# Masked attention on one core: two more groups of a block with three tiles in f16 parts, and VectorE's one-tile gaps on other groups

## What is computed

```python
scores = jnp.einsum('nd,md->nm', x, ks)
scores = jax.nn.leaky_relu(scores, negative_slope=0.2)
scores = jnp.where(adj > 0, scores, -9e15)
attn = jax.nn.softmax(scores, axis=1)
out = layernorm(x + jnp.einsum('nm,md->nd', attn, ks))   # rows of 128, eps 1e-5
```

## Time and profile before

| | |
|---|---|
| median of 3 runs | 1552.41 us |
| profiled execution, own time | 1553.36 us |
| its span, first to last instruction | 1551.6 us |
| granted PE clock, mean | 0.996 |
| busy share of PE, DVE, ACT, POOL | 97%, 97%, 95%, 93% |
| DMA, share of 16 engines | 55.5% |

### The profile page before, as it was taken

The page is one execution under the profiler, slowest core; times in us unless marked ns, Lnnn a source line. Parts: engine busy times, 40 slices in busy tenths (PEclk is TensorE's granted clock), DMA queues, the critical chain, the costliest instruction groups (busy, mean ns, idle before and its releaser), DMA issues.

```text
span 1551.6 us, 43289 instructions
## 1 busy us (share of the span) xinstructions
PE 1502.5 (97%) x16784; PEld 1414.1 (91%) x16784; DVE 1502.6 (97%) x1809; ACT 1475.7 (95%) x1883; POOL 1440.9 (93%) x1245
## 2 busy tenths in 40 slices
PE   5699999999999999999999999999999999999997
PEld 3499999999999999999999999999999999999987
DVE  7999999999999999999999999999999999999984
ACT  6799999999999999999999999999999999999997
POOL 4999999999999999999999999999999999999996
PEclk9999999999999999999999999999999999999999
DMA  9855556555555655555555555655555555555510
GB/s 350 278 194 190 198 197 202 198 188 194 194 192 190 203 190 192 194 192 194 202 191 191 188 187 188 201 183 188 193 190 188 200 182 191 194 188 190 196 63 8
DMA packets 107131, 296.00 MB, mean 191 GB/s; under 512 B 10800, under 2 KB 40240, under 8 KB 106928
## 3 DMA queue, kind: packets, MB, share of 16 engines
q1 hardware_dynamic: 106928, 293.25, 55.5%
HBM read 289.01 MB, written 4.19 MB: 189 GB/s over the span
## 4 chain that ended last, share of the span: by engine, by line
PE 76%; issue 9%; DVE 8%; ACT 5%; POOL 2%; DVEq 0%; DMA 0%; ACTq 0%; POOLq 0%
PE weighted L796 21%; PE scores L748 11%; PE scores L750 11%; PE scores L749 11%; PE weighted L812 7%; PE weighted L808 7%; PE weighted L810 7%; DVE running L654 3%; DVE ring L670 2%; ACT ring L491 2%; DVE ring L640 1%; ACT pt_hi L498 1%; POOL pt_lo L399 1%; ACT scores L484 1%; PE scores L796 0%
## 5 line engine op out<-in xcount | busy, mean ns | idle before, releaser
L394 POOL TENSOR_TENSOR ring<-ring,floor 128x768 f32<-128x768 f32 (+1 forms) x498 | 704.0, 1414 | 48.1 <-ACT floor L511 47.9
L399 POOL TENSOR_TENSOR pt_lo<-ring,pt_hi 128x512 f16<-128x512 f32 (+1 forms) x512 | 658.3, 1286 | 18.1 <-ACT pt_hi L498 17.3
L640 DVE SCALAR_TENSOR_TENSOR ring<-adj_sb,scores 128x1024 f32<-128x1024 int32 x512 | 621.2, 1213 | 6.0 <-ACT scores L484 5.6
L484 ACT ACTIVATE scores<-scores,shrink 128x1024 f32<-128x1024 f32 x512 | 553.6, 1081 | 51.4 <-PE scores L750 46.8
L491 ACT ACTIVATE ring<-ring,lift 128x1024 f32<-128x1024 f32 x512 | 583.6, 1140 | 5.3 <-DVE ring L670 4.0
L748 PE MATMUL scores<-xt_hi,kt_hi 128*128 128x256 f16 x2048 | 560.0, 273 | 25.9 <-DVE ring L640 17.6
L750 PE MATMUL scores<-xt_hi,kt_lo 128*128 128x256 f16 x2048 | 560.5, 274 | 0.0
L749 PE MATMUL scores<-xt_lo,kt_hi 128*128 128x256 f16 x2048 | 560.4, 274 | 0.0
L654 DVE TENSOR_TENSOR running<-ring,running 128x1024 f32<-128x1024 f32 x448 | 547.7, 1223 | 0.1
L796 PE MATMUL weighted<-k_rows,ring 128*128 128x129 f32 x3472 | 472.6, 276 | 2.0 <-DVE y L691 0.9
L796 PEld LDWEIGHTS weighted<-k_rows,ring 128*128 128x128 f32 x3472 | 427.6, 192 | 14.1 <-ACT ring L491 8.1
(11 more groups left out here) (74 smaller groups left out, 544.2 us busy)
## 6 DMA issues: line engine op xcount, KB each, us to landing
adj_sb<-in_adj SPq DMA_DIRECT2D x512, 512.0 KB, 3.4
ring<-in_ks_t SPq DMA_DIRECT2D x8, 512.0 KB, 7.2
x_row<-in_x SPq DMA_DIRECT2D x32, 128.0 KB, 3.5
out<-normed SPq DMA_DIRECT2D x32, 128.0 KB, 3.6
x_probe<-in_x_t SPq DMA_DIRECT2D x29, 128.0 KB, 3.5
xt_raw<-in_x_t SPq DMA_DIRECT2D x29, 128.0 KB, 4.6
ring<-in_ks SPq DMA_DIRECT2D x12, 128.0 KB, 4.8
k_rows<-in_ks SPq DMA_DIRECT2D x12, 128.0 KB, 4.6
```

The source lines that it names most:

```text
L394: nc.gpsimd.tensor_tensor(here, here, below, ALU.subtract).then_inc(gap_ready, 1)
L399: nc.gpsimd.tensor_tensor(pt_lo[:, g % PARTS, 0:QUAD - whole, :], ring[:, g % RING, whole:, :], pt_hi[:, g % PARTS, 0:QUAD - whole, :], AL ...
L640: nc.vector.scalar_tensor_tensor(ring[:, g % RING, :, :], adj_sb[:, g % ADJS, :, :], 0.0, scores[:, g % 2, :, :], ALU.is_le, ALU.subtract)\
```

## The change

Six groups of a block instead of four have three parted tiles: 1, 3, 7, 9, 11 and 15. A block has 38 parted and 26 whole tiles instead of 36 and 28. DVE's one-tile gaps are on groups 0, 5, 8 and 13 instead of 0, 4, 8 and 12. The four portions in which the parts of ks are made follow the table: 10, 9, 10 and 9 tiles instead of 9 each.

```diff
-    WHOLE = [1 if q % 4 == 3 else 2 for q in range(GROUPS)]
+    WHOLE = [1 if q % 8 in (1, 3, 7) else 2 for q in range(GROUPS)]
...
         def dve_tiles(g):
-            return QUAD if g >= ALL - LEFT_OUT else 3 if g >= ALL - GROUPS else min(1 + g % 4, 2)
+            return QUAD if g >= ALL - LEFT_OUT else 3 if g >= ALL - GROUPS else 1 if g % 8 in (0, 5) else 2
...
-                    rows = slice(n * PARTEDS // 4, (n + 1) * PARTEDS // 4)
+                    rows = slice(FIRST_PARTED[4 * n], FIRST_PARTED[4 * n + 4])
```

## The result

The kernel after takes 1558.46 us (median of 6 runs, 1557.94 to 1559.58), the one before, run beside it, 1553.33 us (6 runs, 1552.19 to 1553.93). The ratio is 1.0035, with a 95% interval from 1.0025 to 1.0045: slower by 5.1 us. The prediction was 1552.7 us, no change, and the time lies 2 us above its range (1547.4 to 1556.4). In the profiled execution it took 1558.32 us, with a span of 1556.5 (before 1551.6). The granted clock was 0.995 in the mean, before 0.996. The means are alike, but the two executions have their stretches at the lower clock in different places, and at the end of the program that matters; this is taken up under e6.

A forecast was written before the change was run, and what follows sets the result against it. PE's ring of 46.475 us was taken as the bound, DVE 0.24 behind. Ordinary blocks -0.8, start +0.5 and end +0.6 gave +0.3 us: 1552.7 us on the median, no change, range 1547.4 to 1556.4.

The forecast's parts named there:

- PE's ring: From L683 through a whole block of weigh and score back to L683: 46.475 us, 0.24 longer than DVE's own work.
- the PE step: Two more parted tiles save 0.105 us each in weigh, bringing PE's part of the period to 46.265 us.
- PE, DVE, ACT by themselves: Per block: PE gains 0.21 us, DVE's moved gaps nothing, ACT's longer high parts (0.42 us) hidden by waiting for PE.
- POOL: Two longer low parts cost 0.976 us a block; their lateness lengthens DVE's two-input least, leaving 0.8 us gained of 5.7.
- How late is group 13's low part then?: Overlap of POOL's last low part before the floor wait with DVE's two-input least, put at 0.326 + 46.475 - P.
- P: The period of an ordinary block, from L683 to L683, forecast at 46.45 us.
- PE's lead of 0.21: PE runs 0.21 us ahead of DVE, so the floor starting POOL's next round comes earlier; otherwise the period grows 0.105.
- The start: Two longer low parts in the chain without slack before DVE's first masks: +0.5 us (0 to 0.9).
- The end: After the last mask, where PE waits for POOL's and ACT's longer parts: +0.6 us (0 to 1.2).
- The collision is larger: Slower rival at the two-input least: both unknowns adverse, period 46.68, time 1559.0 us; chance 0.13.
- ACT: Slower rival: masks 7 and 15 wait behind longer high parts, DVE's period 46.66, time 1558.5 us; chance 0.04.
- The gain arrives: Faster rival: POOL's lateness doesn't reach the two-input least, or PE's lead grows; period 46.265, time 1547.8 us; chance 0.23.

The follow-up runs named there:

- e6: The kernel after with L600 (128x3, the last instruction of setting a scale) issued as three of 128x1: 1557.57 us, ratio 1.0024.
- e4: The kernel after, but from the second block on POOL makes only two of three low parts in groups 1 and 9: 1547.64 us, ratio 0.9967.
- e9: e6 with the scaling of each block of x (L365) moved from POOL to ACT: 1550.93 us, ratio 0.9986.
- e7: Against the kernel before: five groups with three parted tiles (1, 3, 7, 11, 15), gaps as before, L600 by columns: 1550.51 us, ratio 0.9981.
- e2: The kernel before with only DVE's one-tile gaps moved to groups 0, 5, 8, 13: 1553.08 us, ratio 1.0000.
- e5: The kernel before, but from the second block on POOL makes three low parts in groups 1 and 9, one unused: 1556.13 us, ratio 1.0021.
- e1: The kernel after with DVE's one-tile gaps on groups 0, 4, 8, 12 as before: 1557.01 us, ratio 1.0030.
- e8: The kernel before with L600 issued as three instructions of 128x1: 1553.81 us, ratio 1.0003.
- e12: e9 with the x scaling of blocks 1 and 2 (counted from 0) left on POOL: 1550.12 us, ratio 0.9985.
- e3: The kernel after, but from the second block on group 1's least takes the running minimum in PSUM instead of group 0 in SBUF: 1549.83 us, ratio 0.9975.

## Why the prediction was wrong

**What bounds the kernel: right.** PE's ring at 46.475 us, DVE just behind: e4 and e9 have the 46.267 that the PE step forecast (46.265), e7 the 46.372 of one tile.

**PE, DVE, ACT by themselves: right.** e2 shows the moved gaps at nothing, e4 the longer high parts of ACT at nothing.

**POOL: the right place and the right mechanism, the sum wrong.** The step that failed is "How late is group 13's low part then?". It counts six terms, overlap = 0.326 + 46.475 - P, and holds DVE by this less 0.14. It lets POOL hold DVE, but not DVE hold POOL. The lengthened `least` ends later, and then overlaps POOL's next gap, which starts 1.19 us after the `least` began, when the floor comes (1188.23 to 1189.42). In the kernel before that was 1.40 (1136.89 to 1138.29), so PE's lead of 0.21 did reach the floor. With s for what the `least` is lengthened by, the gap is longer by (1.225 + s) - 1.19 - 0.14 = s - 0.105. With the measured s = 0.33 that is 0.23: the gap's 2.05 instead of 1.82. This lateness goes once around POOL's round and is there again at the next `least`:

overlap = 0.326 + 46.475 - P + (s - 0.105), and s = overlap - 0.14, so s cancels and P = 46.475 + 0.081 = 46.56 us.

Measured: 46.56. DVE's own 46.235 + s gives s = 0.33, and that too was measured. Read otherwise, two units that exclude each other form one line: POOL's round and the `least` follow each other, and the period is their sum. In my sum half of the excess came back (P stood on both sides and was halved), here none does. That is 0.11 us on P, 27 x 0.11 = 3.0 us of the miss (the 27 periods were put at -0.8 us and came to +2.35). It also shows why the `least` wasn't long in every second block, as I wrote, but about 1.55 in nearly each: a `least` that is longer by s hands on a round that is later by s.

That this second hold makes the rest is read from the traces of after; no experiment took it away alone. The period by itself doesn't tell it from my formula without PE's lead, which gives (93.106 / 2 =) 46.55 us and is what e5 measured; the gap's start at 1.19 us and its 2.05 us do. The trace of before had it too, in the two blocks with a new scale (around 345.8 and 904.9 us), where the gap starts beside the `least`, and I had not looked there:

```profile
345.66 1.22 DVE L654 TENSOR_TENSOR running<-ring 128x1024 f32<-128x1024 f32 x1
345.82 2.73 POOL L394 TENSOR_TENSOR ring<-ring,floor 128x768 f32<-128x768 f32 x1 [1.82 <-ACT floor L511]
```

The `least` still had 1.06 us to run, and the gap took 2.73 us instead of 1.82, 0.91 more.

The Trainium skill (SBUF — State Buffer, Who interferes with whom), which I had cited, has this lock in both directions. It has one line on instructions with two SBUF inputs, as the `least`, and one on DVE's two-port mode, and there it says: "Whoever issues first gets the shared pair for the whole instruction; the other **fully blocks** (not throttle)". I applied it in one direction. The trace agrees in both, but for the 0.14 us in each.

**Left out: L600.** I put the two blocks with a new scale at no change. The three instructions cost 2.3 us more (0.96, 0.69, 0.67), by the same exclusion: in rows before they were already at 0.54 where one column takes 0.21, and I hadn't looked for what else DVE has that a low part can hold. e6 shows the shape as the cause (all at 0.21). The Trainium skill (VectorE: DVE Perf Modes, What auto-detection actually checks) bears on it: a one-source operation from SBUF to SBUF goes in the two-port mode when the outermost non-unit dimensions are both even or equal, as three and three are; 128x1 has no such dimension. The runs agree, though they show the shape and not the mode. One thing differs from "whoever issues first": by the start times of the trace all three L600 began 0.01 to 0.02 us ahead of POOL's low part (345.70 and 345.72), and it was DVE that was held.

**The start** was put at +0.5, for POOL's longer low parts; without L600 it is 1.74 - 0.96 = +0.78. But e1 has these low parts too, and its first L683 is only 122.44 - 122.08 = 0.36 later, 0.24 of it by L600. So the low parts alone cost 0.1 there, and the size came near only together with the moved gaps, which alone (e2, 122.35) cost 0.3 at most. **The end** was put at +0.6 and came to -0.46. That was no fault of the term: at a clock of 1.00 the stretch takes 77.75 us with the work of before (e2) and 78.58 now, +0.8, and PE waits 5.2 us for low parts there in place of the 4.5 of the earlier trace rows. The difference of -1.3 is the lower clock that the profiled execution of before had there.

```profile
PE weighted L808 <- POOL pt_lo L399: 5.2, 5, 2.0
```

**The sum by the mended steps:** 2.4 (27 x 0.087) + 2.3 (L600) + 0.8 (start) + 0.8 (end) - 1.3 (clock of before at its end) = +5.0 us, against the 4.96 of the two spans and the 5.1 of the runs. Only the first term is worked out; the others are what the traces show. At the full clock in both ends the loss would be some 6 us (an estimate from e2, e8 and after); the shortest runs, 1551.43 us of before at a clock of 0.999 and 1557.94 of after at 0.998, are 6.5 apart. The rival "The collision is larger" had 1559.0 us, near the time but by the wrong road: it needed P = 46.68, with PE's lead not reaching the floor, and no L600. Its place was right, the two-input `least`. The rivals ACT (e4) and "The gain arrives" fell; the latter is what e4 shows once POOL is as short as before.

**What stays open:** why the longer low parts and the moved gaps together cost 0.8 us at the start, where apart they cost 0.1 and 0.3. The clock doesn't tell it: between 40 and 80 us it was 0.91 in e6 and 1.00 in e12, and both have the first L683 at 123.10 us. Open too is what lowers the clock at the end of some executions.

## What to carry to other kernels

Where two engines exclude each other, write the cycle as one line and let the delay go both ways: a delay that comes back undiminished cancels out of the equation, and the period is then set by the sum of both, as here. Before work is given to an engine with slack in the waits view, look where in the round this slack lies and what the other engine does in it: here 1.55 us of slack covered 0.49 us more (e7), but not 0.98. Compare the minimum and the maximum of each small instruction by its shape; a short one that is sometimes long was held here, and the waits view didn't list it. And where two profiles are compared, compare the granted clock stretch by stretch: the means here were 0.995 and 0.996, and the end still differed by 1.3 us.

## What the runs showed of the hardware

- The exclusion of DVE and POOL is mutual and nearly exact. DVE held by POOL: an overlap of 0.47 us cost 0.33; in the second block of after a `least` with 1.58 us of overlap took 2.68 instead of 1.23:

```profile
62.80 2.28 POOL L380 TENSOR_TENSOR k_parts<-ring,k_parts 128x1152 f16<-128x1152 f32 x1
...
63.50 2.68 DVE L654 TENSOR_TENSOR running<-ring 128x1024 f32<-128x1024 f32 x1
```

  POOL held by DVE: an overlap of 0.37 us cost 0.23, one of 1.06 us in the trace of before cost 0.91. In all four the price is the overlap less 0.13 to 0.15 us.
- It appears as a longer duration and not as idle time, so neither the waits view nor the releasers name it; DVE's busy time even rises, from 1502.6 to 1511.2 us.
- A DVE instruction of 128x3 f32 with SBUF on both sides was held for up to 1.0 us (1.23 instead of 0.23); as three of 128x1, 0.21 us each, it never was (e6).
- With one input in PSUM the same `least` took 1.22 us beside POOL's subtraction, in all groups of e3 from the second block on.
- At the end of the program a granted clock of 0.91 or 0.87 between 1500 and 1520 us, instead of 1.00, went with an end that was 0.7 to 1.6 us longer for the same work (e2 and before; e12, e9 and e6).
